# Sixteen pairs of heads in one line: making the next pair's keys and values beside the scores, and writing the maxima into the score banks with ScalarE

## The chip, the core and the metric

The kernel runs on one core of a Trainium2 chip. Its time is the device time of one execution in microseconds. The core has five engines that work side by side and meet only at semaphores: TensorE (PE in the profile) multiplies matrices, VectorE (DVE), ScalarE (ACT) and GpSimd (POOL) work on elements, and SyncE (SP) issues the transfers. TensorE writes to the eight banks of PSUM, each 512 float32 wide on 128 partitions; GpSimd cannot read them, DVE and ACT can.

## The reference, cut to what matters

The whole computation is a four-layer model with cross attention, self attention and a feed-forward part in each layer. The change touches only the cross attention of layer 1: 2 batches of 256 latent rows attend to 4096 context rows and to the latents themselves, with 16 heads of width 64.

```python
x = layer_norm(x, ln_m_g, ln_m_b)                # context: 2 x 4096 x 256
lat = layer_norm(latents, ln_l_g, ln_l_b)        # 2 x 256 x 256
q = lat @ Wq                                     # 256 -> 1024 = 16 heads of 64
kv = jnp.concatenate([x, lat], axis=1) @ Wkv     # 4352 keys and values
k, v = jnp.split(kv, 2, axis=-1)
q, k, v = (split_heads(q), split_heads(k), split_heads(v))
dots = jnp.einsum('bhid,bhjd->bhij', q, k) * scale
attn = jax.nn.softmax(dots, axis=-1)
out = jnp.einsum('bhij,bhjd->bhid', attn, v)
return out.transpose(0, 2, 1, 3).reshape(b, m, heads * dim_head) @ Wout
```

## The kernel before, in words

`latent_attention` (L1324) does the part between the queries and the normalized averages. It loops twice over the batch (`Fori`, L1363), each turn of the loop a stage of its own with a barrier at its end. In a turn there are four groups of four heads, that is, of two pairs of heads; a pair fills the 128 partitions with two heads of 64. A group has two phases.

In the **fill phase** TensorE makes 18 key tiles (`tile`, L1474: two pairs of heads, nine blocks of up to 512 keys) and 17 value tiles (L1479: 256 keys by four heads). ACT copies each out of PSUM (L1588, L1591). GpSimd casts the keys to bfloat16 (L1410). Between the tiles TensorE makes coarse scores from bfloat16 keys and queries (`peak_products`, L1453) into two sets of two banks, and DVE reduces each set to the maximum of every query (`read_peaks`, L1629). The maxima of a pair of heads are turned into a row by TensorE (`peak_rows`, L1492), and DVE copies the row to `mrow` (L1639).

In the **score phase** the group has 34 steps, 17 for each pair of heads, taken two at a time. A step has 256 keys: TensorE first writes the negative maxima into two score banks with two bfloat16 matmuls of a row of ones and `mrow` (L1509), adds the float32 scores on top (L1515), ACT takes the exponential over 1024 columns (L1605), and TensorE multiplies the result by the values (`average`, L1532). DVE (L1651) and GpSimd (L1421) each add one head's exponentials up, and at a pair's end TensorE sums them over partitions (`denominators`, L1545). `normalize` (L1658, L1659) divides. The averages of the preceding two steps come behind the scores of the present two.

The order is written out by hand, engine by engine. The score banks `pss` hold the tiles of the fill phase too, so the two phases of a group cannot overlap. In front of all this a small stage clears `mrow` (L1352), and each turn of the loop begins with 20 idle matmuls (`keep_busy`, L106). Afterwards `project_residual` (L309) multiplies by the output weights.

Of the kernel before, what the change touches and what calls it, by code (L numbers as in the profile page):

```python
# [14 lines left out]
ALU = mybir.AluOpType  # L15
# [1308 lines left out]
def latent_attention(nc, k, d, pre, OT):  # L1324
# [3 lines left out]
    hd, KEYS, GROUPS, RING = HD64, CTX + S, 4, 4  # L1328
    KT = KEYS // P
    SCALE = float(hd) ** -0.5  # L1330
    NQ = [(j * 512, min(512, KEYS - j * 512)) for j in range((KEYS + 511) // 512)]
    NB = len(NQ)
    NK, NV = KC * NB, KT // 2
    TILES = NK + NV
    STEPS = KT // 2
    ALL = KC * STEPS
    PEAKS = KC * NB
    QEV = 2 * KC

    names = ("c_load0 c_load1 c_load2 c_load3 latents nt_here wq_load wk_load wv_load q_mm q_ev tile_mm tile_ev k_cast peaks peak_read peak rows row_in "  # L1340
             "scored exps averaged sum_dve sum_pool den o_done chain").split()
    with Tensors(nc) as t:
        cT = t.sb(pre + "_cT", [P, KC, KEYS])
        V = t.sb(pre + "_V", [P, KT, 4, hd])
        K = t.sb(pre + "_K", [P, KC, KEYS])
        Kb = t.sb(pre + "_Kb", [P, KC, KEYS], BF16)
        Qb = t.sb(pre + "_Qb", [P, 2, KC, S], BF16)
        mrow = t.sb(pre + "_mrow", [P, KC, 2, S], BF16)
        with stage(nc, pre + "_fill", pre + "_fill1") as (block, _u, _v):
            @block.gpsimd  # L1350
            def _(pool):
                nc.gpsimd.memset(mrow[:, :, :, :], 0.0)  # L1352

        with nc.Fori(0, B) as b:
            with Tensors(nc) as u, stage(nc, *[pre + "_" + n for n in names], repeated=True) as (block, *sems):
                (c_load0, c_load1, c_load2, c_load3, latents, nt_here, wq_load, wk_load, wv_load, q_mm, q_ev, tile_mm, tile_ev, k_cast, peaks, peak_read, peak, rows, row_in,
                 scored, exps, averaged, sum_dve, sum_pool, den, o_done, chain) = sems
                c_loads = (c_load0, c_load1, c_load2, c_load3)
                CL = CTX // 4
                w = u.sb(pre + "_w", [P, 3, KC, D])  # L1360
                nt = u.sb(pre + "_nt", [P, KC, S])
                Q = u.sb(pre + "_Q", [P, 2, KC, S])
                pk = u.sb(pre + "_pk", [P, KC, QT, 2, NB])  # L1363
                mx = u.sb(pre + "_mx", [P, KC, 4])
                acc = u.sb(pre + "_acc", [P, 2, 2, 2, S])
                pr = u.sb(pre + "_pr", [P, RING, 2, 2, S])
                rec = u.sb(pre + "_rec", [P, S])
                pss = u.ps(pre + "_pss", [P, 4, 512])
                psm = u.ps(pre + "_psm", [P, 2, 512])
                pso = u.ps(pre + "_pso", [P, 512])  # L1370
                pst = u.ps(pre + "_pst", [P, 512])

                def averages_of(n):
                    return pso[:, 0:S] if n == 0 else psm[:, 1, 0:S]

                def peaks_by(t_):

                    if t_ < 2:
                        return 0
                    return min(PEAKS, -(-PEAKS * (t_ - 1) // (TILES - 2)))  # L1380

                def peak_banks(qt):
                    return psm[:, :, :] if qt == 0 else pss[:, 2:4, :]

                @block.sync
                def _(sp):
                    for g in range(GROUPS):
                        if g >= 1:
                            sp.wait_ge(q_mm, g)
                        sp.dma_start(w[:, 0, :, :], d[pre + "_w3"][g][:, 0]).then_inc(wq_load, 16)  # L1390
                        if g >= 1:
                            sp.wait_ge(tile_mm, TILES * (g - 1) + NK)
                        sp.dma_start(w[:, 1, :, :], d[pre + "_w3"][g][:, 1]).then_inc(wk_load, 16)
                        if g == 0:
                            for x in range(4):
                                sp.dma_start(cT[:, :, x * CL:(x + 1) * CL], k.normedT[b][:, :, x * CL:(x + 1) * CL]).then_inc(c_loads[x], 16)
                        if g >= 1:
                            sp.wait_ge(tile_mm, TILES * g)
                        sp.dma_start(w[:, 2, :, :], d[pre + "_w3"][g][:, 2]).then_inc(wv_load, 16)

                @block.gpsimd
                def _(pool):
                    nc.gpsimd.tensor_copy(nt[:, :, :], k.NT[:, :, bass.ds(b * S, S)]).then_inc(nt_here, 1)
                    nc.gpsimd.tensor_copy(cT[:, :, CTX:KEYS], k.NT[:, :, bass.ds(b * S, S)]).then_inc(latents, 1)
                    for g in range(GROUPS):
                        for n in range(NK):
                            m, j = divmod(n, NB)
                            o, w_ = NQ[j]
                            pool.wait_ge(tile_ev, TILES * g + n + 1)
                            nc.gpsimd.tensor_copy(Kb[:, m, o:o + w_], K[:, m, o:o + w_]).then_inc(k_cast, 1)  # L1410
                        for a in range(ALL):
                            n, s = divmod(a, STEPS)
                            A, U = ALL * g + a, KC * g + n
                            pool.wait_ge(exps, A + 1)
                            if s == 0:
                                if U >= 2:
                                    pool.wait_ge(den, U - 1)
                                i = nc.gpsimd.tensor_copy(acc[:, n, 1, :, :], pr[:, A % RING, :, 1, :])
                            else:
                                pool.wait_ge(sum_pool, A)  # L1420
                                i = nc.gpsimd.tensor_tensor(acc[:, n, 1, :, :], acc[:, n, 1, :, :], pr[:, A % RING, :, 1, :], ALU.add)  # L1421
                            i.then_inc(sum_pool, 1)

                @block.tensor
                def _(pe):
                    def queries(g):
                        pe.wait_ge(wq_load, 16 * (g + 1))
                        if g == 0:
                            pe.wait_ge(nt_here, 1)
                        else:  # L1430
                            pe.wait_ge(peak_read, QT * PEAKS * g)
                        for m in range(KC):
                            for c in range(KC):
                                i = nc.tensor.matmul(psm[:, 0, m * S:(m + 1) * S], w[:, 0, c, m * P:(m + 1) * P], nt[:, c, :],
                                                     start=(c == 0), stop=(c == KC - 1))
# [2647 lines left out]
```

## Time and profile before

| what | value |
|---|---|
| median of 3 runs | 3688.89 us (3686.14 to 3690.83) |
| span of the profiled execution | 3677.2 us |
| median less span | 11.7 us |
| the changed part: first queries to the last denominators' end | 599.12 to 1812.25 us |
| TensorE busy in the span | 92% |

The profiled execution's own time is given only as its span, from the first instruction to the last; the median of the timed runs lies 11.7 us above it. "Granted clock" is the share of TensorE's full clock that the chip let it have in a stretch. Busy time of TensorE is modelled: a matmul's duration covers its way through the array, so the distance between the starts of two groups of matmuls says what one costs, and the duration printed does not. A float32 matmul shows as two records.

### The profile page before, as it was taken

To read this page: it belongs to the slowest core of one execution; us is meant where nothing else is said; L and a number is where in the kernel's file an instruction comes from. 1 tells how busy PE (TensorE), PEld (TensorE's weight loads), DVE (VectorE), ACT (ScalarE), POOL (GpSimd) and SP (SyncE) were. 2 spreads that over 40 slices of the span, in tenths; PEclk is the share of its full clock that TensorE was granted. 3 is DMA by queue.
4 is the path that set the end of the run, shared out by engine and by line. 5 is a ranking of instruction groups with operands and counts; after the bars stand their busy time and mean duration, and the time that the engine had idled before them with its cause. 6 is when DMAs were issued, how large, how long until landed. Compare 5 with 4: busy or idle time off the path is not lost. (4 is left out here: it accounts for less than half of the span.)

```text
span 3677.2 us, 56678 instructions
## 1 busy us (share of the span) xinstructions
PE 3396.7 (92%) x22589; PEld 2130.7 (58%) x22608; DVE 2126.4 (58%) x3378; ACT 1525.3 (41%) x2294; POOL 904.2 (25%) x665
## 2 busy tenths in 40 slices
PE   8989898999999999999967888999988889999899
PEld 5855695655656556565634576444455644445575
DVE  4335313555555555555468621999855279995654
ACT  2335211424334243343355522466745137665621
POOL 1032001426345163452517512000011120000430
PEclk9999999999999999999988999999999989999999
DMA  5358562000000100000097533756500386550010
GB/s 190 105 188 273 186 249 84 7 6 5 7 1 1 61 7 9 4 4 1 12 241 281 206 143 120 190 117 121 101 26 24 124 226 125 117 106 22 1 48 36
DMA packets 228860, 346.91 MB, mean 94 GB/s; under 512 B 104176, under 2 KB 177584, under 8 KB 223984
## 3 DMA queue, kind: packets, MB, share of 16 engines
q1 hardware_dynamic: 228208, 342.16, 32.1%
q8 instruction: 184, 3.01, 0.3%
q0 software_dynamic: 384, 1.05, 0.1%
q14 instruction: 84, 0.69, 0.1%
HBM read 257.15 MB, written 86.02 MB: 93 GB/s over the span
## 5 line engine op out<-in xcount | busy, mean ns | idle before, releaser
L1421 POOL TENSOR_TENSOR L1x_acc<-L1x_acc,L1x_pr 128x512 f32<-128x512 f32 x256 | 418.0, 1633 | 135.7 <-ACT L1x_pr L1605 117.4
L1605 ACT ACTIVATE L1x_pr<-L1x_pss 128x1024 f32<-128x1024 f32 x272 | 278.4, 1024 | 288.2 <-PE L1x_pss L1515 280.5
L1651 DVE TENSOR_TENSOR L1x_acc<-L1x_acc,L1x_pr 128x512 f32<-128x512 f32 x256 | 255.4, 997 | 213.2 <-ACT L1x_pr L1605 209.4
L1234 DVE TENSOR_REDUCE L3x_pk<-L3x_psm 128x1 f32<-128x512 f32 x512 | 328.8, 685 | 25.9 <-PE L3x_psm L1063 19.4
L1234 DVE TENSOR_REDUCE L2x_pk<-L2x_psm 128x1 f32<-128x512 f32 x512 | 328.8, 685 | 20.7 <-PE L2x_psm L1063 14.1
L1211 ACT ACTIVATE L3x_pr<-L3x_pss 128x1024 f32<-128x1024 f32 x256 | 248.1, 1021 | 106.3 <-PE L3x_pss L1106 106.0
L1211 ACT ACTIVATE L2x_pr<-L2x_pss 128x1024 f32<-128x1024 f32 x256 | 248.1, 1021 | 102.0 <-PE L2x_pss L1106 101.8
L1629 DVE TENSOR_REDUCE L1x_pk<-L1x_psm 128x2 f32<-128x1024 f32 x144 | 168.0, 1167 | 211.1 <-PE L1x_psm L1453 211.1
L1515 PE MATMUL L1x_pss<-L1x_Q,L1x_K 64*128 64x256 f32 x2176 | 279.3, 376 | 0.0
L1479 PE MATMUL L1x_pss<-L1x_w,L1x_cT 128*128 128x256 f32 x1088 | 257.5, 387 | 0.0
L1474 PE MATMUL L1x_pss<-L1x_cT,L1x_w 128*128 128x512 f32 (+1 forms) x576 | 256.4, 584 | 0.5 <-DMA L1x_cT<-normed_context 0.5
L1479 PEld LDWEIGHTS L1x_pss<-L1x_w,L1x_cT 128*128 128x128 f32 x1088 | 200.1, 190 | 54.6 <-issue 27.2
L1515 PEld LDWEIGHTS L1x_pss<-L1x_Q,L1x_K 64*128 64x128 f32 x2176 | 208.4, 188 | 36.0
L2894 POOL TENSOR_SCALAR s_qz<-s_qT,s_mask 128x256 f32<-128x256 f32 x64 | 58.3, 918 | 652.1 <-SPq L58 433.8
L3876 POOL TENSOR_TENSOR o_pr<-o_h,m_cr 128x1024 f32<-128x1024 f32 x31 | 72.8, 2355 | 504.1 <-DVE o_h L3955 504.1
L1588 ACT COPY L1x_K<-L1x_pss 128x512 f32<-128x512 f32 x144 | 80.8, 561 | 257.5 <-PE L1x_pss L1474 257.5
L1474 PEld LDWEIGHTS L1x_pss<-L1x_cT,L1x_w 128*128 128x128 f32 x576 | 102.4, 189 | 120.8 <-issue 110.2
L1591 ACT COPY L1x_V<-L1x_pss 128x512 f32<-128x512 f32 x136 | 79.6, 585 | 217.9 <-PE L1x_pss L1479 217.9
L1629 DVE TENSOR_REDUCE L1x_pk<-L1x_pss 128x2 f32<-128x1024 f32 x144 | 166.5, 1156 | 0.0
L841 PE MATMUL n_psk<-n_cT,n_w 128*128 128x512 f32 x256 | 125.7, 616 | 37.0 <-DMA n_cT<-in_ctxT 36.9
L879 ACT ACTIVATE n_kst<-n_psk,n_b 128x512 bf16<-128x512 f32 x192 | 121.6, 688 | 57.3 <-PE n_psk L841 47.7
L1410 POOL CAST L1x_Kb<-L1x_K 128x512 bf16<-128x512 f32 x144 | 84.9, 590 | 242.8 <-ACT L1x_K L1588 242.8
(742 smaller groups left out, 6126.7 us busy)
## 6 DMA issues: line engine op xcount, KB each, us to landing
f0e_wt<-in_f_pieces SPq DMA_DIRECT2D x10, 3072.0 KB, 11.5
offset_rows<-s_rows SPq DMA_DIRECT2D x32, 768.0 KB, 5.8
L2x_KS<-L2x_key_parts SPq DMA_DIRECT2D x24, 1024.0 KB, 12.8
L3x_KS<-L3x_key_parts SPq DMA_DIRECT2D x24, 1024.0 KB, 12.8
s_add<-offset_rows SPq DMA_DIRECT2D x32, 512.0 KB, 7.5
n_cT<-in_ctxT SPq DMA_DIRECT2D x32, 512.0 KB, 4.6
f1e_wt<-in_f_pieces SPq DMA_DIRECT2D x8, 2048.0 KB, 12.7
L2x_key_parts<-n_kst SPq DMA_DIRECT2D x32, 384.0 KB, 2.8
```

The costliest lines, as they stand in the source:

```text
L841: i = nc.tensor.matmul(cx.psk[:, n % 4, :], cx.w[:, l, 0, c, m * P:(m + 1) * P], cx.cT[:, q % CRING, c, :], start=(c == 0), stop=(c == KC ...
L879: nc.scalar.activation(cx.kst[:, q % SRING, m, part, :], cx.psk[:, n % 4, :], ACT.Identity, bias=cx.bias[:, mine[q][1], m:m + 1]).then_inc ...
L1211: nc.scalar.activation(pr[:, a % RING, :, :].rearrange("p h q -> p (h q)"), pss[:, 2 * (a % 2):2 * (a % 2) + 2, :].rearrange("p x q -> p ( ...
L1234: nc.vector.reduce_max(pk[:, n % 2, h * QT + qt, j:j + 1], psm[:, x % 3, :], AX).then_inc(turn_read, 1)
L1410: nc.gpsimd.tensor_copy(Kb[:, m, o:o + w_], K[:, m, o:o + w_]).then_inc(k_cast, 1)
L1421: i = nc.gpsimd.tensor_tensor(acc[:, n, 1, :, :], acc[:, n, 1, :, :], pr[:, A % RING, :, 1, :], ALU.add)
L1474: i = nc.tensor.matmul(pss[:, x, 0:w_], w[:, 1, c, m * P:(m + 1) * P], cT[:, c, o:o + w_], start=(c == 0), stop=(c == KC - 1))
L1479: i = nc.tensor.matmul(pss[:, x, c * D:(c + 1) * D], cT[:, e, kt * P:(kt + 1) * P], w[:, 2, e, :], start=(e == 0), stop=(e == KC - 1))
L1515: i = nc.tensor.matmul(pss[:, x + h, e * S:(e + 1) * S], K[half, n, kt * P:(kt + 1) * P], Q[half, g % 2, n, :], start=False, stop=True, sk ...
L1605: nc.scalar.activation(pr[:, A % RING, :, :, :].rearrange("p h e q -> p (h e q)"), pss[:, x:x + 2, :].rearrange("p h n -> p (h n)"), ACT.E ...
L1629: nc.vector.reduce_max(pk[:, m, qt, :, j], peak_banks(qt)[:, :, 0:NQ[j][1]], AX).then_inc(peak_read, 1)
L1651: i = nc.vector.tensor_tensor(acc[:, n, 0, :, :], acc[:, n, 0, :, :], pr[:, A % RING, :, 0, :], ALU.add)
```

## The change

`latent_attention` is written anew as one stage without the loop. The eight groups of both batches form one line of 136 pairs of steps. Beside each pair of steps TensorE now makes one key tile (11 tiles ahead of use, `KLEAD`), one value tile (9 ahead, `VLEAD`) and the coarse scores of one key tile. The last key blocks of two pairs of heads share one tile (`KL`), so a group has 17 key tiles. The two bfloat16 matmuls that wrote the maxima are gone: TensorE spreads the negative maxima over all partitions once for each pair of heads (`spread_rows`, a matmul of ones with diagonal matrices that DVE makes), ACT copies them to `neg`, and `seed` has ACT write `neg` into the two score banks before each step. The key tile has PSUM bank 0 of `psm`, the value tile bank 2; the coarse scores of the first 128 queries use banks 0 and 1, those of the other 128 banks 1 and 2. The small clearing stage is gone.

```diff
-    hd, KEYS, GROUPS, RING = HD64, CTX + S, 4, 4
-        with nc.Fori(0, B) as b:
-                def averages_of(n):
-                    return pso[:, 0:S] if n == 0 else psm[:, 1, 0:S]
+    hd, RING, GROUPS = HD64, 4, B * 4
+    KLEAD, VLEAD, VRING, BRING = 11, 9, SLOTS + 2, 3
+        def read_in(p):
+            z = p + KLEAD - 1
+            return z if z < TILES else None
+        def peak_banks(z, qt):
+            return psm[:, qt:qt + 2, :] if z >= KLEAD - 1 else pss[:, 2 * qt:2 * qt + 2, :]
...
# TensorE
-                        for h in range(2):
-                            half = slice(64 * h, 64 * h + 64)
-                            nc.tensor.matmul(pss[:, x + h, :], k.onesb[half, :], mrow[half, n, :, :].rearrange("p e q -> p (e q)"),
-                                             start=True, stop=False, skip_group_check=True)
+            def spread_rows(u, bank):
+                pe.wait_ge(diag, u + 1)
+                nc.tensor.matmul(psm[:, bank, :], k.onesb[:, :], dm[:, :, :, :].rearrange("p h t q -> p (h t q)"), start=True, stop=True).then_inc(rows, 1)
+            def scores(a):
+                u, s = unit_of(a)
+                g, m = divmod(u, KC)
+                pe.wait_ge(seeded, a + 1)
...
+            for z in range(KLEAD):
+                key_tile(z)
+                if z >= KLEAD - VLEAD:
+                    value_tile(z - KLEAD + VLEAD)
+                if z >= 1:
+                    pe.wait_ge(k_cast, z)
...
+                    for qt in range(QT):
+                        peak_products(z - 1, qt)
+            pe.wait_ge(k_ev, KLEAD - 1)
+            spread_rows(0, 1)
+            for p in range(PAIRS):
+                z = read_in(p)
+                def first_peaks():
+                    if z is not None:
+                        pe.wait_ge(k_cast, z + 1)
+                        pe.wait_ge(peak_read, QT * z)
...
+                        peak_products(z, 0)
+                def second_peaks():
+                    if z is not None:
+                        pe.wait_ge(peak_read, QT * z + 1)
+                        pe.wait_ge(v_ev, VLEAD + 1 if p == 0 else min(TILES, p + VLEAD))
...
+                        peak_products(z, 1)
+                def tiles():
+                    if keys_in(p) is not None:
+                        key_tile(keys_in(p))
+                    if values_in(p) is not None:
+                        if p >= 1:
+                            pe.wait_ge(peak_read, QT * min(TILES, p + KLEAD))
+                        value_tile(values_in(p))
...
+                first_peaks()
+                scores(2 * p)
+                scores(2 * p + 1)
+                second_peaks()
+                if p > 0:
+                    tiles()
...
+                for a in averages_in(p):
+                    average(a)
# ScalarE
+            def seed(a):
...
+                nc.scalar.copy(pss[:, x:x + 2, :].rearrange("p h (e q) -> p h e q", e=2),
+                               neg[:, u % 2, :, :].unsqueeze(2).broadcast_to([P, 2, 2, S])).then_inc(seeded, 1)
...
+                exponentials(2 * p)
+                exponentials(2 * p + 1)
+                if p + 1 < PAIRS:
+                    act.wait_ge(exps, 2 * p + 1)
+                    seed(2 * p + 2)
+                if p > 0 and keys_in(p) is not None:
+                    evict_keys(keys_in(p))
+                if p + 1 < PAIRS:
+                    act.wait_ge(exps, 2 * p + 2)
+                    seed(2 * p + 3)
+                if p > 0 and values_in(p) is not None:
+                    evict_values(values_in(p))
# GpSimd
+            for p in range(PAIRS):
+                sum_step(2 * p)
+                sum_step(2 * p + 1)
+                if keys_in(p) is not None:
+                    cast(keys_in(p))
# VectorE
+            for p in range(PAIRS):
+                z = read_in(p)
+                if z is not None:
+                    read_peaks(z, 0)
...
+                if z is not None:
+                    read_peaks(z, 1)
+                    diagonals(z)
+                sum_step(2 * p)
+                sum_step(2 * p + 1)
```

This is TensorE's line before, in the score phase of a group. `L1x_pss` are the score banks, `mrow` the maxima, `pr` the exponentials.

```order
L1509 MATMUL L1x_pss<-L1x_mrow,ones_bf 128x512 x2
L1515 MATMUL L1x_pss<-L1x_Q,L1x_K 128x256 x4
L1509 MATMUL L1x_pss<-L1x_mrow,ones_bf 128x512 x2
L1515 MATMUL L1x_pss<-L1x_Q,L1x_K 128x256 x4
L1532 MATMUL L1x_pso<-L1x_pr,L1x_V 64x256 x8
```

These five rows are one pair of steps; the tiles stand in another stretch of the same line. This is TensorE's line after, one pair of steps in the middle of the line and the first two rows of the next. `L1x_psm` holds tiles and coarse scores.

```order
L1525 MATMUL L1x_psm<-L1x_Kb,L1x_Qb 128x512 x2
L1542 MATMUL L1x_pss<-L1x_Q,L1x_K 128x256 x8
L1525 MATMUL L1x_psm<-L1x_Kb,L1x_Qb 128x512 x2
L1501 MATMUL L1x_psm<-L1x_cT,L1x_w 128x512 x2
L1516 MATMUL L1x_psm<-L1x_w,L1x_cT 128x256 x4
L1555 MATMUL L1x_pso<-L1x_pr,L1x_V 64x256 x8
L1525 MATMUL L1x_psm<-L1x_Kb,L1x_Qb 128x512 x2
L1542 MATMUL L1x_pss<-L1x_Q,L1x_K 128x256 x8
```

The writing of the maxima is gone from TensorE, and coarse scores (L1525), a key tile (L1501) and a value tile (L1516) stand inside every pair of steps. On ScalarE a group was this before, 18 key copies, 17 value copies and then 34 exponentials without anything between them:

```order
L1588 COPY L1x_K<-L1x_pss 128x512 x8
L1588 COPY L1x_K<-L1x_pss 128x256
L1588 COPY L1x_K<-L1x_pss 128x512 x8
L1588 COPY L1x_K<-L1x_pss 128x256
L1591 COPY L1x_V<-L1x_pss 128x512 x17
L1605 ACTIVATE L1x_pr<-L1x_pss 128x1024 x34
```

One pair of steps on ScalarE now, with the exponentials of the next pair behind it:

```order
L1671 ACTIVATE L1x_pr<-L1x_pss 128x1024 x2
L1661 COPY L1x_pss<-L1x_neg 128x1024
L1646 COPY L1x_K<-L1x_psm 128x512
L1661 COPY L1x_pss<-L1x_neg 128x1024
L1650 COPY L1x_V<-L1x_psm 128x512
L1671 ACTIVATE L1x_pr<-L1x_pss 128x1024 x2
```

Two copies over 1024 columns into PSUM (L1661) are new in each pair of steps, and the two tile copies stand between and behind them.

## Rows read from the trace of the kernel before

**Rows 1.** The page: busy time and share of the span of each engine.

```profile
PE 3396.7 (92%) x22589; PEld 2130.7 (58%) x22608; DVE 2126.4 (58%) x3378; ACT 1525.3 (41%) x2294; POOL 904.2 (25%) x665
```

**Rows 2.** Windows: stretch, length, busy of PE, PEld, DVE, ACT, POOL, granted clock.

```profile
600.00:676.00 76.00, 73.56 (x295) 40.87 (x294) 43.80 (x46) 20.05 (x35) 10.62 (x18) 1.00 0.13 50
676.00:753.00 77.00, 76.95 (x642) 49.37 (x644) 39.14 (x42) 35.98 (x36) 54.70 (x36) 1.00 0.03 8
```

**Rows 3.** Timeline (start, duration, engine) of TensorE: one pair of steps.

```profile
689.46 1.95 PE L1532 MATMUL L1x_pso<-L1x_pr,L1x_V 128*64 128x256 f32 x16
691.34 0.39 PE L1509 MATMUL L1x_pss<-L1x_mrow,ones_bf 64*128 64x512 bf16 x2
691.57 1.03 PE L1515 MATMUL L1x_pss<-L1x_Q,L1x_K 64*128 64x256 f32 x8
...
693.61 1.95 PE L1532 MATMUL L1x_pso<-L1x_pr,L1x_V 128*64 128x256 f32 x16
```

**Rows 4.** Timeline of TensorE: fill phase, value tiles and coarse scores.

```profile
656.78 3.72 PE L1479 MATMUL L1x_pss<-L1x_w,L1x_cT 128*128 128x256 f32 x16
660.43 0.39 PE L1453 MATMUL L1x_psm<-L1x_Kb,L1x_Qb 64*128 64x512 bf16 x2
...
660.97 3.72 PE L1479 MATMUL L1x_pss<-L1x_w,L1x_cT 128*128 128x256 f32 x16
```

**Rows 5.** Timeline of TensorE: from the first turn of the loop to the second.

```profile
1199.00 2.27 PE L106 MATMUL L1x_pss<-ident 128*128 128x128 f32 x18
...
1213.12 1.89 PE L1434 MATMUL L1x_psm<-L1x_nt,L1x_w 128*128 128x256 f32 x8
1214.85 5.31 PE L1474 MATMUL L1x_pss<-L1x_cT,L1x_w 128*128 128x512 f32 x12
1220.10 0.39 PE L1453 MATMUL L1x_psm<-L1x_Kb,L1x_Qb 64*128 64x512 bf16 x2
```

**Rows 6.** Timeline of all engines: a wait of TensorE for DVE's reads.

```profile
606.86 0.39 PE L1453 MATMUL L1x_psm<-L1x_Kb,L1x_Qb 64*128 64x512 bf16 x2
607.29 1.23 DVE L1629 TENSOR_REDUCE L1x_pk<-L1x_psm 128x2 f32<-128x1024 f32 x1 [4.82 <-PE L1x_psm L1453]
608.43 1.22 DVE L1629 TENSOR_REDUCE L1x_pk<-L1x_pss 128x2 f32<-128x1024 f32 x1
609.79 0.39 PE L1453 MATMUL L1x_psm<-L1x_Kb,L1x_Qb 64*128 64x512 bf16 x2 [0.42 <-DVE L1x_pk L1629]
```

**Rows 7.** Timeline of all engines: exponentials and sums of two steps.

```profile
885.82 1.03 PE L1515 MATMUL L1x_pss<-L1x_Q,L1x_K 64*128 64x256 f32 x8
886.89 2.10 ACT L1605 ACTIVATE L1x_pr<-L1x_pss 128x1024 f32<-128x1024 f32 x2 [2.04 <-PE L1x_pss L1515]
887.95 0.69 DVE L1651 TENSOR_TENSOR L1x_acc<-L1x_acc,L1x_pr 128x512 f32<-128x512 f32 x1 [1.77 <-ACT L1x_pr L1605]
888.00 3.45 POOL L1421 TENSOR_TENSOR L1x_acc<-L1x_acc,L1x_pr 128x512 f32<-128x512 f32 x2 [0.69 <-ACT L1x_pr L1605]
```

**Rows 8.** Tile `L1x_acc`: durations in ns, least, median, greatest.

```profile
L1651 DVE TENSOR_TENSOR L1x_acc<-L1x_acc,L1x_pr x256: 691/693/1579, 679.4 to 1808.7; 128x512 f32<-128x512 f32 x128
L1421 POOL TENSOR_TENSOR L1x_acc<-L1x_acc,L1x_pr x256: 1263/1536/1786, 679.5 to 1809.6; 128x512 f32<-128x512 f32 x128
```

**Rows 9.** Groups by line: tile copies, casts.

```profile
L1410 POOL CAST L1x_Kb<-L1x_K 128x512 bf16<-128x512 f32 x144 | 84.9, 590 | 242.8 <-ACT L1x_K L1588 242.8
L1588 ACT COPY L1x_K<-L1x_pss 128x512 f32<-128x512 f32 x144 | 80.8, 561 | 257.5 <-PE L1x_pss L1474 257.5
```

**Rows 10.** Timeline: the small stage, the start and the end of the changed part.

```profile
591.54 0.95 POOL L1352 MEMSET L1x_mrow<- 128x1024 bf16 x1 [15.10 <-POOLq L58]
...
599.12 1.89 PE L1434 MATMUL L1x_psm<-L1x_nt,L1x_w 128*128 128x256 f32 x8
...
601.53 5.39 PE L1474 MATMUL L1x_pss<-L1x_cT,L1x_w 128*128 128x512 f32 x12 [0.52 <-DMA L1x_cT<-normed_context]
...
1812.25 2.27 PE L106 MATMUL L1x_pss<-ident 128*128 128x128 f32 x18
```

More of the change, by code:

```diff
@@ L1324, in latent_attention @@
 def latent_attention(nc, k, d, pre, OT):
-    hd, KEYS, GROUPS, RING = HD64, CTX + S, 4, 4
-    KT = KEYS // P
-    SCALE = float(hd) ** -0.5
[L1331 to L1341, printed above, removed]
@@ new lines, in latent_attention @@
+    hd, RING, GROUPS = HD64, 4, B * 4
+    UNITS = KC * GROUPS
+    KT = (CTX + S) // P
+    STEPS = KT // 2
+    NBLK = CTX // 512
+    SLOTS = STEPS
+    ALL = STEPS * UNITS
+    PAIRS, TILES = ALL // 2, SLOTS * GROUPS
+    KLEAD, VLEAD, VRING, BRING = 11, 9, SLOTS + 2, 3
+    SCALE = float(hd) ** -0.5
+    OF_W = 16 * 3
+    names = ("c_here0 c_here1 c_here2 c_here3 c_here4 c_here5 c_here6 c_here7 w_here q_mm q_ev k_mm k_ev v_mm v_ev k_cast peaks peak_read diag rows row_in "
+             "seeded scored exps averaged o_copied sum_dve sum_pool den den_read o_done chain").split()
```

621 lines of the change are left out of this document (319 added, 302 removed).

## The prediction

> **What bounds the kernel now.** I read the page first: TensorE is busy 92% of the span, no other engine above 58% [rows 1]. The windows of the changed part say the same of each phase: in a fill phase TensorE is busy 73.6 of 76 us at granted clock 1.00 (the upper level, 2.4 GHz), in a score phase 76.95 of 77 us; ACT has 20 and 36 us, DVE 44 and 39, GpSimd 11 and 55 [rows 2]. So TensorE bounds both phases, and the change is worth what it takes from TensorE's line, provided that no other engine becomes late in the new, denser order. The rows are then read by the distance between starts, because that is what a piece costs on TensorE.
>
> **What the pieces cost.** A pair of steps takes 693.61 - 689.46 = 4.15 us: averages A 1.88, and 2.27 for two times maxima and scores. One writing of maxima is 691.57 - 691.34 = 0.23, so the scores S of two steps take 2.27 - 0.46 = 1.81, with a change of array mode behind them [rows 3]. The coarse scores P of one block take 660.97 - 660.43 = 0.54, which is two pieces of 0.23 and 0.08 for the change from 64-row mode to whole-array mode [rows 4]. Eight whole-array records followed by others of that mode take 1214.85 - 1213.12 = 1.73 (a key tile has the same number of columns; three of them with the change behind take 5.25, or 1.75 each) [rows 5]. Two value tiles take 660.43 - 656.78 = 3.65 with the change behind, so a last value tile V takes 1.92 [rows 4].
>
> **A pair of steps after the change.** P in two parts 0.54, S 1.73 (1.81 less the 0.08 for a change of mode that no longer follows, since P's second part has the scores' mode), key tile K 1.73, V 1.92, A 1.88: 7.80 us. By the old phases, without looking at joints, it would be 4.15 - 0.46 + 0.54 + 3.65 = 7.88. The cheapest reading drops the change between V and A, 1.73 in place of 1.92: 7.61. I take 7.80.
>
> The trace prices a change of array mode at 0.08 us behind coarse scores and 0.19 behind value tiles [rows 4, 5]. The Trainium skill, TensorEngine Tiling (Array Packing), Key Properties, says that changing the mode drains TensorE. It speaks against a line that changes mode inside every pair. By it one counts: before, two changes in a score pair and two around a coarse block, four; after, A to P, P to K and V to A, three. The Trainium skill has no price for it; without the rule the sum would go by 7.88 and end 10 us higher, at 3589.
>
> **Does anything else get late inside 7.80 us?** Let a pair start at 0 with P's first part. S runs 0.23 to 1.96, P's second part to 2.27, K to 4.00, V to 5.92, A to 7.80.
> - *DVE.* The second part of P shares a bank with the first and waits for its read. A read starts 0.43 after the matmuls, takes 1.23, and TensorE goes on 0.14 after its end (607.29 - 606.86; 609.79 less 608.43 + 1.22) [rows 6]: 1.80, against 1.96, a slack of 0.16. V waits likewise: 1.96 + 1.80 = 3.76 against 4.00. Then come two sums of 0.69 to 1.58 [rows 8], done by 3.62 + 3.16 = 6.8 at the latest. It is the tightest place.
> - *ACT.* An exponential starts 1.07 after its scores' first matmul and takes 1.05 (886.89 - 885.82, two in 2.10) [rows 7]: 1.30 to 3.40, in time for A at 5.92. The two seeds have no row: ACT writes nothing into PSUM before. Below, the half-width copy out of PSUM, 0.56 [rows 9]; above, the dearest element work of that kind at full width, twice an exponential, 2.1; I take 1.05, since the exponential has the same 128x1024 [rows 7]. Then seed to 4.45, key copy to 5.0, seed to 6.1, value copy to 6.7. The second scores of the next pair want the second seed at 7.80 + 1.10 = 8.9: seeds up to 2.4 us cost nothing, so neither end of that bound is on the path.
> - *GpSimd.* Two sums take 3.45 [rows 7] from 2.37 on, to 5.8, the cast 0.59 [rows 9], to 6.4. The next pair's P waits for that cast at 7.80. Slack 1.4.
> - *SP* brings the second batch's context in eight parts, each seven or more pairs (55 us) before its key tile, so the wait at the loop's second turn goes. No DMA is queued behind another that is due sooner.
> - Diagonals of DVE (16 times), the queries' copies and the copy of the denominators have a pair's slack each; I cost them at nothing, and at most 0.5 us x 32 = 16 us if they meet P's read.
>
> **The sum, from first queries to last denominators.** Queries and the wait for the context 2.4 (601.53 - 599.12) [rows 10]. Ahead of the first scores 11 K, 9 V, 10 P: 1.73, 2.46 and 9 x 4.19, 41.9. Hand-over: one matmul that spreads the row, K, V, and a wait for ACT, which makes two seeds only after the last coarse read: reads end 2.8 after P's start, seeds 2.1, key copy 0.6, against 0.54 + 0.3 + 3.65 of TensorE: 1.2; together 5.2. The rest of pair 0: 4.2. Pairs 1 to 124: 124 x 7.80 = 967.2. Pair 125 has no K, 6.1, pair 126 no K and P, 5.5. The last nine have scores and averages only, 3.6 of TensorE, but ACT has two exponentials and two seeds, 4 x 1.05 + 0.1: 9 x 4.3 = 38.7; 2.0 for the last averages. Seven more queries of 1.73, 12.1; 16 denominators at half of A, 15.0; 15 spread rows of 0.25, 3.8. Total 1104.1 us. Before it is 1812.25 - 599.12 = 1213.1 [rows 10]. Difference -109.0. The clearing stage (a memset of 0.95) goes, -1.0; its bounds are 0 and -2. At the end the denominators are copied by ACT before the reciprocal, +0.5. In all -109.5.
>
> Where it comes from: 272 writings of maxima of 0.23 (62), the loop's seam of 1213.12 - 1199.00 = 14.1 [rows 5], the coarse blocks reduced by eight and the rows made by eight small matmuls (about 10), the fill phases' own waits (the 76 - 73.6 of a fill, eight times, 19), a change of mode per pair (10), less what ACT holds up at the end (6) and the hand-over.
>
> The span would be 3677.2 - 109.5 = 3567.7. The profiled execution's own time is not given beside its span; the median is 11.7 above the span, so the forecast is **3579 us**.
>
> **Rivals.**
> - *The reads of the maxima wait in view.* The slack of 0.16 is a difference of modelled ends. If a read starts late or takes longer beside ACT's writes, P's second part and V wait. At +0.35 per pair: 125 x 0.35 = 44, 3623. For it: DVE already made TensorE wait 0.42 there, though in another order [rows 6]. Against it: in a pair DVE has 5.6 us at the most for 7.8.
> - *The joints are cheap.* A pair of 7.61: 125 x 0.19 = 24 less, 3555. For it: whole-array and column-split mode may follow each other without a loss, which no row shows by itself; against it: A itself shows 1.88 where its columns match 1.73.
> - *GpSimd slowed by DVE: slower.* GpSimd's sums grow, since DVE is now busy most of the time, and the cast, queued behind both sums on GpSimd, comes late for P, on whose heels everything hangs. It decides from 7.80 - 2.37 - 0.59 - 0.1 = 4.7 us for two sums on; the kernel is slower than before from a pair of 7.80 + 109.5 / 124 = 8.68 on, that is, sums of 2.8 each. At 3.3 each the pair is 9.66: 125 x 1.86 = 232 more, less 109.5, 3811. For it: GpSimd's sums range from 1.26 to 1.79 and DVE's from 0.69 to 1.58 beside each other [rows 8]. Against it: 1.79 is the most in 256, with both at work. The Trainium skill, SBUF — State Buffer, Who interferes with whom, says that a DVE instruction with at most one SBUF input outside its two-port modes does not contend with GpSimd, while one with two does. The added DVE work beside the sums is reads of PSUM, so by the Trainium skill this rival is nearly out; the trace has no reads beside GpSimd's sums to show it.
> - *It is not what it says:* ACT's own waits between exponential and seed (it waits for its own exponential's end) could cost some tenths each, but ACT has 2.4 us free per pair; that leaves 3579 as it is, but for the last nine pairs, +3.
>
> **Chances.** Forecast 0.74 (own range 3565 to 3597, pairs of 7.70 to 7.93), reads in view 0.13, joints cheap 0.08, GpSimd 0.03, something not seen 0.02. The range 3558 to 3622 leaves out GpSimd's case and the far half of the first rival. A measurement of this kernel can tell 0.2%, 7.4 us, from no change. Faster: 0.95; same 0.01; slower 0.04.
>
> **What would show it.** In the timeline of the new kernel pairs start 7.7 to 7.9 apart, TensorE is busy over 97% from the first key tile to pair 126, at clock 1.00, ACT copies of 128x1024 into the score banks take 1.0 to 1.1, nobody waits for them before the last nine pairs, and those are 4.3 apart. Waits of TensorE put down to DVE's reduction of more than 0.1 each would show the first rival; waits put down to GpSimd's cast, the third. The forecast is wrong if pairs are over 8.0 apart or the last nine far over 4.3.

## The result, and the profile after

The changed kernel takes 3577.78 us (median of 4; 3571.99 to 3585.08) against 3687.51 us (4 runs) before: a ratio of 0.971, 95% interval 0.9695 to 0.9724, 110 us less. Forecast were 3579 us. Timed again beside the experiments it was 3580.21, ratio 0.970 (0.9685 to 0.9716).

The windows of the profile after: ahead of the changed part, the part from its first queries to its last denominators, and behind it (columns as in [rows 2], then DMA share and GB/s).

```profile
0.00:602.59 602.59, 533.72 (x3131) 407.46 (x3131) 222.85 (x619) 173.27 (x381) 83.49 (x92) 0.97 0.54 187
602.59:1709.68 1107.09, 1095.87 (x6800) 693.54 (x6800) 698.07 (x718) 688.57 (x848) 492.36 (x408) 1.00 0.04 13
1709.68:3583.30 1873.62, 1689.28 (x11966) 1008.78 (x11964) 1243.69 (x2073) 910.87 (x1360) 301.52 (x152) 0.95 0.44 117
```

The part takes 1107.1 us, 106.0 less than the 1213.1 between the rows of before [rows 10]; 1104.1 were forecast. TensorE is busy for 99% of it at clock 1.00, ACT for 62% (688.6). A pair of steps in the middle of the line, in the timeline of all engines but TensorE's weight loads:

```profile
1011.86 0.39 PE L1525 MATMUL L1x_psm<-L1x_Kb,L1x_Qb 64*128 64x512 bf16 x2
1012.09 1.89 PE L1542 MATMUL L1x_pss<-L1x_Q,L1x_K 64*128 64x256 f32 x16
1012.30 1.23 DVE L1730 TENSOR_REDUCE L1x_pk<-L1x_psm 128x2 f32<-128x1024 f32 x1 [0.18 <-PE L1x_psm L1525]
1013.17 1.94 ACT L1671 ACTIVATE L1x_pr<-L1x_pss 128x1024 f32<-128x1024 f32 x2 [2.49 <-PE L1x_pss L1542]
1013.82 0.38 PE L1525 MATMUL L1x_psm<-L1x_Kb,L1x_Qb 64*128 64x512 bf16 x2
1014.13 1.98 PE L1501 MATMUL L1x_psm<-L1x_cT,L1x_w 128*128 128x512 f32 x4
1014.27 2.94 POOL L1464 TENSOR_TENSOR L1x_acc<-L1x_acc,L1x_pr 128x512 f32<-128x512 f32 x2 [3.81 <-ACT L1x_pr L1671]
1014.99 1.03 ACT L1661 COPY L1x_pss<-L1x_neg 128x1024 f32<-128x1024 f32 x1
1015.38 2.38 DVE L1760 TENSOR_TENSOR L1x_acc<-L1x_acc,L1x_pr 128x512 f32<-128x512 f32 x2
1015.95 1.89 PE L1516 MATMUL L1x_psm<-L1x_w,L1x_cT 128*128 128x256 f32 x8
1016.15 0.58 ACT L1646 COPY L1x_K<-L1x_psm 128x512 f32<-128x512 f32 x1
1016.63 1.02 ACT L1661 COPY L1x_pss<-L1x_neg 128x1024 f32<-128x1024 f32 x1
1017.16 1.07 POOL L1450 CAST L1x_Kb<-L1x_K 128x512 bf16<-128x512 f32 x1
1017.77 1.95 PE L1555 MATMUL L1x_pso<-L1x_pr,L1x_V 128*64 128x256 f32 x16
1019.65 0.39 PE L1525 MATMUL L1x_psm<-L1x_Kb,L1x_Qb 64*128 64x512 bf16 x2
```

Read the starts of TensorE's rows: 0.23 for P's first part, 1.73 for the scores, 0.31, key tile 1.82, value tile 1.82, averages 1.88, in all 7.79. No row of TensorE carries a wait in brackets. ACT's two seeds (L1661) stand ahead of the key copy and behind it, 1.03 and 1.02, and its next exponential comes 2.5 us after its last work. Where [rows 3] had 0.23 twice per pair for the maxima, there is nothing on TensorE.

The hand-over from the lead to the first pairs, and the last pairs, in TensorE's timeline:

```profile
646.11 0.39 PE L1531 MATMUL L1x_psm<-L1x_dm,ones_bf 128*128 128x512 bf16 x1
...
650.92 0.39 PE L1525 MATMUL L1x_psm<-L1x_Kb,L1x_Qb 64*128 64x512 bf16 x2 [0.98 <-ACT L1x_K L1646]
...
653.74 2.00 PE L1555 MATMUL L1x_pso<-L1x_pr,L1x_V 128*64 128x256 f32 x16 [0.49 <-ACT L1x_pr L1671]
...
657.06 0.39 PE L1525 MATMUL L1x_psm<-L1x_Kb,L1x_Qb 64*128 64x512 bf16 x2 [1.32 <-POOL L1x_Kb L1450]
...
1657.99 1.99 PE L1516 MATMUL L1x_psm<-L1x_w,L1x_cT 128*128 128x256 f32 x8 [1.32 <-DVE L1x_pk L1730]
...
1681.89 2.00 PE L1542 MATMUL L1x_pss<-L1x_Q,L1x_K 64*128 64x256 f32 x16
1684.15 2.00 PE L1555 MATMUL L1x_pso<-L1x_pr,L1x_V 128*64 128x256 f32 x16 [0.26 <-ACT L1x_pr L1671]
1686.08 2.00 PE L1542 MATMUL L1x_pss<-L1x_Q,L1x_K 64*128 64x256 f32 x16
```

Pair 0 waits three times, 2.8 us in all. Pair 125 has no key tile between P's second part and its value tile, and there the wait for DVE's read comes into view, 1.32. The last pairs are 1686.08 - 1681.89 = 4.19 apart.

### The profile page after: what moved, and what is told of

It reads as the page before. It is cut to its first block and busy times, and to the rows that moved or that the text cites. A ratio compares the mean times of both kernels' runs of the same rounds, so it can differ in the third digit from the quotient of the medians.

```text
span 3583.3 us, 56143 instructions
## 1 busy us (share of the span) xinstructions
PE 3318.9 (93%) x21894; PEld 2109.8 (59%) x21894; DVE 2164.6 (60%) x3410; ACT 1772.7 (49%) x2589; POOL 877.4 (24%) x652
## 3 DMA queue, kind: packets, MB, share of 16 engines
q0 software_dynamic: 384, 1.05, 0.1%
## 5 line engine op out<-in xcount | busy, mean ns | idle before, releaser
L1464 POOL TENSOR_TENSOR L1x_acc<-L1x_acc,L1x_pr 128x512 f32<-128x512 f32 x256 | 357.6, 1397 | 538.6 <-ACT L1x_pr L1671 521.4
L1730 DVE TENSOR_REDUCE L1x_pk<-L1x_psm 128x2 f32<-128x1024 f32 x238 | 291.7, 1226 | 318.9 <-PE L1x_psm L1525 318.9
L1661 ACT COPY L1x_pss<-L1x_neg 128x1024 f32<-128x1024 f32 x272 | 278.5, 1028 | 1.3 <-DVE L1x_pk L1730 1.3
L1555 PE MATMUL L1x_pso<-L1x_pr,L1x_V 128*64 128x256 f32 x2176 | 265.3, 386 | 2.6 <-ACT L1x_pr L1671 2.6
L1501 PE MATMUL L1x_psm<-L1x_cT,L1x_w 128*128 128x512 f32 x512 | 253.4, 618 | 0.0
L1516 PE MATMUL L1x_psm<-L1x_w,L1x_cT 128*128 128x256 f32 x1024 | 242.0, 379 | 1.3 <-DVE L1x_pk L1730 1.3
L1516 PEld LDWEIGHTS L1x_psm<-L1x_w,L1x_cT 128*128 128x128 f32 x1024 | 194.5, 190 | 79.0 <-issue 30.2
L1555 PEld LDWEIGHTS L1x_pso<-L1x_pr,L1x_V 128*64 128x64 f32 x2176 | 143.4, 136 | 107.1 <-issue 40.7
L1501 PEld LDWEIGHTS L1x_psm<-L1x_cT,L1x_w 128*128 128x128 f32 x512 | 87.0, 189 | 113.1 <-issue 112.8
L1106 PE MATMUL L2x_pss<-L2x_QS,L2x_KS 97*128 97x256 bf16 x1024 | 138.1, 277 | 0.6
```

Of the source, the lines that this page charges most:

```text
L1106: i = nc.tensor.matmul(pss[:, 2 * (a % 2) + h // 2, h % 2 * S:(h % 2 + 1) * S], KS[0:ONE + 1, n % 2, h, s * P:(s + 1) * P], QS[0:ONE + 1, ...
L1501: i = nc.tensor.matmul(psm[:, x, :], w[:, g % 2, 1, c, m * P:(m + 1) * P], cT[:, c, j * 512:(j + 1) * 512], start=(c == 0), stop=(c == KC ...
L1516: i = nc.tensor.matmul(psm[:, 2, h * D:(h + 1) * D], keys, w[:, g % 2, 2, c, :], start=(c == 0), stop=(c == KC - 1))
L1555: i = nc.tensor.matmul(pso[64 * h:64 * h + 64, 0:S], V[:, (SLOTS * g + s) % VRING, e, 2 * n + h, :], pr[:, a % RING, h, e, :], start=(s == ...
L1661: nc.scalar.copy(pss[:, x:x + 2, :].rearrange("p h (e q) -> p h e q", e=2), neg[:, u % 2, :, :].unsqueeze(2).broadcast_to([P, 2, 2, S])).t ...
L1730: nc.vector.reduce_max(pk[:, m, qt, :, j], peak_banks(z, qt), AX).then_inc(peak_read, 1)
```

## The experiments

The theory: TensorE bounds every full pair; the seeds gain because they leave TensorE where ACT has room; the seam and the fill phases' waits make up the rest. Lengths of the part are read from each run's trace as above (first queries to last denominators' end); they repeat closely (1107.1 in both profiles of the changed kernel), while the rest of the program varies by 20 us from one profiled execution to another (2458.8 to 2479.1). Each ratio is taken to the kernel before as timed beside that run (3684.05 to 3687.77 us). Edits are shown in part; `...` in them marks lines left out.

| run | us | ratio to before (95%) | length of the part |
|---|---|---|---|
| before | 3687.51 | | 1213.1 |
| changed | 3577.78 | 0.971 (0.9695 to 0.9724) | 1107.1 |
| e0 changed, again | 3580.21 | 0.97 (0.9685 to 0.9716) | 1107.1 |
| e1 line, maxima by TensorE | 3631.75 | 0.9852 (0.9835 to 0.987) | 1158.4 |
| e2 two phases, seeds, half the maxima of a group's first steps lost | 3699.54 | 1.0032 (1.0021 to 1.0044) | 1231.3 |
| e2b the same, all maxima kept | 3707.4 | 1.0054 (1.0033 to 1.0074) | 1230.9 |
| e3 DVE's read late | 3587.87 | 0.9731 (0.971 to 0.9752) | 1119.4 |
| e4 seeds twice | 3608.23 | 0.9783 (0.9754 to 0.9811) | 1140.2 |
| e5 a line per batch | 3599.38 | 0.9765 (0.9742 to 0.9788) | 1128.1 |
| e6 both ends changed | 3581.22 | 0.9712 (0.9694 to 0.9729) | 1108.8 |
| e7 GpSimd late | 3724.68 | 1.011 (1.0085 to 1.0135) | 1255.1 |
| e8 tail: averages late, DVE seed | 3579.05 | 0.9697 (0.9679 to 0.9716) | 1107.9 |
| e9 tail: averages late | 3580.43 | 0.971 (0.969 to 0.973) | 1106.9 |

**The changed kernel again.** 

> The changed kernel once more, beside the others on the same chip. Expected 3573 to 3585 us, as in its four runs; the distance between its time and its span 1.8 us as in them, which would put the 11.7 us of the prediction down to the spread between executions.

It came as expected; its profiled execution took 3581.13 us with a span of 3579.4, so 1.7 us lie around the span.

**e1: half of the change, the line without the seeds.**

```diff
-                pe.wait_ge(seeded, a + 1)
...
+                if a >= 2:
+                    pe.wait_ge(exps, a - 1)
+                for h in range(2):
+                    half = slice(64 * h, 64 * h + 64)
+                    nc.tensor.matmul(pss[:, 2 * (a % 2) + h, :], k.onesb[half, :], mrow[half, u % 2, :, :].rearrange("p e q -> p (e q)"),
+                                     start=True, stop=False, skip_group_check=True)
...
```

> The changed line, but the maxima are written into the score banks by two bfloat16 matmuls per step again, and ACT makes no seeds (half of the change). Theory: TensorE bounds every pair, so 272 x 0.23 = 62 us come back, less about 1 at the hand-over; pairs 8.24 apart in place of 7.78; 3638 us. Rival: overlap is what gained and the seeds on ACT only kept even; then 3578 to 3590.

Two pairs' first rows in TensorE's timeline:

```profile
1036.35 0.39 PE L1526 MATMUL L1x_psm<-L1x_Kb,L1x_Qb 64*128 64x512 bf16 x2
1036.57 0.38 PE L1543 MATMUL L1x_pss<-L1x_mrow,ones_bf 64*128 64x512 bf16 x2
...
1044.56 0.39 PE L1526 MATMUL L1x_psm<-L1x_Kb,L1x_Qb 64*128 64x512 bf16 x2
```

8.21 apart, 0.43 more than 7.78: 125 such pairs are 54 us, and the part is 51.3 longer; 3638 us was expected and 3631.75 measured. The 14 pairs with a row of maxima grow only from 8.35 to 8.53. The theory's mechanism holds, at 0.22 a step in place of 0.23; the rival, that the seeds only kept even, falls.

**e2 and e2b: the other half alone, seeds in the two-phase kernel.**

```diff
# TensorE's scores
...
-                            nc.tensor.matmul(pss[:, x + h, :], k.onesb[half, :], mrow[half, n, :, :].rearrange("p e q -> p (e q)"),
-                                             start=True, stop=False, skip_group_check=True)
+                        pe.wait_ge(seeded, ALL * g + a + 1)
# ScalarE, behind each second exponential
+                            if a % 2 == 1 and a + 1 < ALL:
+                                act.wait_ge(exps, A)
+                                seed(g, a + 1)
+                                act.wait_ge(exps, A + 1)
+                                seed(g, a + 2)
# e2b only: the value tile's second half starts without the flag
-                                                         start=(e == 0), stop=(e == KC - 1))
+                                                         start=(e == 0 and c == 0), stop=(e == KC - 1), skip_group_check=True)
...
```

> The kernel before with its loop and its two phases, but ACT writes the maxima into the score banks (the other half of the change). Theory: a pair of steps of the score phase has 3.7 us of TensorE, but two exponentials and two seeds on ACT, 4.19, which is what a pair takes before (4.15); the seeds gain nothing there, and each group adds a seed of 1.03 between the last tile and the first scores: 3690 us, from 3685 to 3700. Rival: what leaves TensorE is gained wherever it leaves: 62 us less, 3626.

> The kernel of e2 with one flag changed so that the first steps of a group keep their maxima (in e2 half the columns of each group's first steps lost them); the work and its order are the same. Theory: the same time as e2, 3697 to 3707, slower than the kernel before by 10 to 20 us, with pairs 4.12 apart; what TensorE no longer does there is not gained. Rival: the lost maxima had changed the time; then another number than e2's.

The timeline of all engines in e2b, first scores of a group and, further down, a pair in the middle:

```profile
678.54 1.96 ACT L1569 COPY L1x_pss<-L1x_neg 128x1024 f32<-128x1024 f32 x2
679.61 2.08 PE L1496 MATMUL L1x_pss<-L1x_Q,L1x_K 64*128 64x256 f32 x16 [1.72 <-ACT L1x_pss L1569]
...
683.73 3.68 PE L1496 MATMUL L1x_pss<-L1x_Q,L1x_K 64*128 64x256 f32 x16 [2.04 <-ACT L1x_pss L1569]
...
707.66 2.00 PE L1496 MATMUL L1x_pss<-L1x_Q,L1x_K 64*128 64x256 f32 x16
708.84 1.94 ACT L1598 ACTIVATE L1x_pr<-L1x_pss 128x1024 f32<-128x1024 f32 x2 [1.99 <-PE L1x_pss L1496]
710.66 1.97 ACT L1569 COPY L1x_pss<-L1x_neg 128x1024 f32<-128x1024 f32 x2
711.75 2.07 PE L1496 MATMUL L1x_pss<-L1x_Q,L1x_K 64*128 64x256 f32 x16 [0.21 <-ACT L1x_pss L1569]
```

Pairs of plain score steps are 4.11 to 4.12 apart, as good as the 4.15 of before [rows 3]: 0.45 us less of TensorE's work is given back as waits for ACT: 0.2 ahead of the scores of each pair, and 0.2 again for the weight loads of the second step. At a group's start TensorE waits 1.72 and 2.04 in the group shown. From the last value tile's start to the first averages' start a group takes 9.84 to 11.45 us, against 7.32 in all eight before: about 24 us more in sum, where one seed of 1.03 for each group, 8 us, was expected. That is most of why 3707.4 us came out and not 3690. The lost maxima of e2 changed nothing in the time of the part (1231.3 and 1230.9).

The edit has one more piece: the last coarse block of a pair of heads is 512 keys wide in place of 256, which by the distance from the block to the next value tile (0.53 in place of 0.32) makes an estimated 3 us (16 x 0.21) of the 18 by which the part is longer. So the seeds are worth +14 to +18 us in the two phases and -51 us in the line (1107.1 against 1158.4).

**e3: a later read by DVE.**

```diff
+                if z >= KLEAD and qt == 0:
+                    nc.vector.tensor_copy(spare[:, :], psm[:, 0, 0:S])
                 if j < NBLK:
```

> The changed kernel with one more DVE copy of 128x256 out of PSUM (0.34 us from start to next start) ahead of the read that the second part of the coarse scores waits for, in each of the 125 pairs. If the slack of that read is the 0.15 us that the trace shows, each pair grows by 0.19: 24 us, 3602, and the second part of P waits for DVE in every pair. Rival: the slack is larger than its modelled ends say: 3578. Or there is none, and all 0.34 show: 3621.

TensorE and DVE in one pair:

```profile
1009.47 0.39 PE L1526 MATMUL L1x_psm<-L1x_Kb,L1x_Qb 64*128 64x512 bf16 x2
...
1010.24 1.22 DVE L1733 TENSOR_REDUCE L1x_pk<-L1x_psm 128x2 f32<-128x1024 f32 x1
...
1011.52 0.39 PE L1526 MATMUL L1x_psm<-L1x_Kb,L1x_Qb 64*128 64x512 bf16 x2
```

P's second part starts 2.05 after the first, in place of 1.96, and 0.06 after the read's end. The pair is 7.88 to 7.89, 0.10 longer, and the part 12.3. Of the 0.34 added 0.24 were slack: the slack was real, small, and larger than the 0.15 expected, so that 3587.87 us came out in place of 3602. The changed kernel's own rows agree: the read ends at 1013.53 and P's second part starts at 1013.82; less the 0.06 that is 0.23.

**e4: seeds twice.**

```diff
+                nc.scalar.copy(pss[:, x:x + 2, :].rearrange("p h (e q) -> p h e q", e=2),
+                               neg[:, u % 2, :, :].unsqueeze(2).broadcast_to([P, 2, 2, S])).then_inc(once, 1)
+                act.wait_ge(once, a + 1)
                 nc.scalar.copy(...).then_inc(seeded, 1)
```

> The changed kernel with each seed written twice by ACT, one after the other. Theory: up to 2.4 us a seed costs nothing beside a full pair, so pairs stay 7.78 apart; only the last nine pairs grow, by 2.1 to 2.3 each, and the hand-over by 2 to 3: 3600 us. Rival: ACT is near the path already and the pairs grow by 1 us or more: 3700 and up.

```profile
1014.22 0.39 PE L1525 MATMUL L1x_psm<-L1x_Kb,L1x_Qb 64*128 64x512 bf16 x2
...
1017.34 1.03 ACT L1661 COPY L1x_pss<-L1x_neg 128x1024 f32<-128x1024 f32 x1
...
1018.41 1.02 ACT L1664 COPY L1x_pss<-L1x_neg 128x1024 f32<-128x1024 f32 x1
...
1022.00 0.39 PE L1525 MATMUL L1x_psm<-L1x_Kb,L1x_Qb 64*128 64x512 bf16 x2
```

The plain pairs stay at 7.78 to 7.80: two more microseconds of ACT beside them are free. The part is 33.1 longer, not 22: pairs with one more duty on the row of maxima come to 8.84 in place of 8.35 (14 of them, 7 us), seven with denominators to 9.36 in place of 8.65 (5 us). From pair 125 on it takes 72.1 in place of 55.4, 16.7 more, with plain tail pairs at 6.2; the other 4 or so are at the start, from the first queries to pair 2.

**e5: a line per batch.**

```diff
+    for b in range(B):
+        one_line(nc, k, d, pre, OT, b)
...
-    hd, RING, GROUPS = HD64, 4, B * 4
+    hd, RING, GROUPS = HD64, 4, 4
```

> The changed kernel, but the line is cut into two of 8 head pairs, one for each batch, each a stage with its own lead and its own end. Theory: the seam costs about what it cost before, 14 us, and a second hand-over (2.8), a second set of nine pairs bound by ACT (5) come with it: 22 us, 3600. Rival: the single line is the larger part of the gain: 3630 and up.

```profile
1156.46 2.27 PE L106 MATMUL L1x_pss<-ident 128*128 128x128 f32 x18
1159.57 4.70 PE L106 MATMUL L1x_pss<-ident 128*128 128x128 f32 x40 [0.83 <-PEq L58]
1164.11 1.89 PE L1481 MATMUL L1x_psm<-NT,L1x_w 128*128 128x256 f32 x8
1167.18 3.67 PE L1500 MATMUL L1x_psm<-L1x_cT,L1x_w 128*128 128x512 f32 x8 [1.18 <-DMA L1x_cT<-normed_context]
```

The part is 21.0 longer, where 22 were expected. The seam itself is 7.7 us (1164.11 - 1156.46), about half of what the loop's took [rows 5]; a wait for the context (1.18), a second hand-over and a second tail make up the rest, more than was expected for them, so the total came right with its parts off. In the one line the seam costs nothing: with what comes along it is 21 of the 106 us.

**e7: GpSimd late.**

```diff
+                    for e in range(2):
+                        nc.gpsimd.tensor_tensor(spare[:, e, :, :], k.NT[:, 0, :].rearrange("p (e q) -> p e q", e=2), k.NT[:, 1, :].rearrange("p (e q) -> p e q", e=2), ALU.add)
                     cast(keys_in(p))
```

> The changed kernel with two more additions of 128x512 on GpSimd (1.0 to 1.5 us each) between its sums and the cast in each of the 125 pairs. By the trace the cast has 1.3 us to spare; so each pair grows by 0.7 to 1.7, 90 to 210 us: 3670 to 3790 us, and the coarse scores wait for the cast. Rival: the cast is not waited for so closely and nothing changes, 3578.

GpSimd and TensorE at the end of a pair:

```profile
1062.56 2.95 POOL L1475 TENSOR_TENSOR L1x_spare<-NT 128x512 f32<-128x512 f32 x2
1065.46 0.61 POOL L1451 CAST L1x_Kb<-L1x_K 128x512 bf16<-128x512 f32 x1
...
1066.12 0.39 PE L1528 MATMUL L1x_psm<-L1x_Kb,L1x_Qb 64*128 64x512 bf16 x2 [1.03 <-POOL L1x_Kb L1451]
```

Plain pairs are mostly 8.88 apart, 1.10 longer (some others reach 10.5 to 12.1, so that the part is 148 longer), and the kernel is slower than before. That is the forecast's slower rival made by hand: past the cast's slack everything added on GpSimd is added to the time. The 2.9 us added, less 1.4 of slack (the cast ends at 1018.23, P starts at 1019.65) and the 0.46 by which the cast became shorter, are 1.1.

**e6, e8, e9: the ends.**

```diff
# e6: GpSimd casts the next key tile ahead of the first sums; ACT copies it out between the first two seeds;
# in the last nine pairs:
+                if TAIL <= 2 * p + 3 < ALL:
+                    seed_by_dve(2 * p + 3)
...
# e9: averages a pair late in the last pairs; e8: that, and seed_by_dve in the last six
+            if p >= PAIRS - 7:
+                return [2 * p - 2, 2 * p - 1] if p > PAIRS - 7 else []
```

> The changed kernel with its two ends mended: at the hand-over GpSimd casts the next key tile before the first sums and ACT copies it out between the two seeds, and in the last nine pairs DVE makes the second seed. Theory: pair 0 loses about 1 us in place of 2.8, the last nine pairs come down from 4.19 to about 3.8: 5 us less than the changed kernel, 3573, too little to be told from it in the times but visible in the trace. Rival: DVE's seed takes longer than ACT's and the last nine stay at 4.2 or rise.

> The changed kernel with two edits in its last pairs: the averages stand behind the next pair's scores (as in the kernel before), and DVE makes the second seed. After e6, where the last pairs kept 4.19 us though ACT had 1.33 free, the theory is that they are bound by a chain: scores, first exponential, averages, next scores, on TensorE in that order. With the averages a pair late the chain is broken, and with a seed taken from ACT TensorE's own 3.7 us are left: about 0.45 us less in each of the last six pairs, 3 us, 3577. Rival: something else holds these pairs and they stay at 4.19.

> The same with the averages late alone; ACT makes both seeds. Theory: the chain is broken, but ACT's own four instructions take 1.94 + 1.97 and two joints, so the last pairs come to 4.0 to 4.1 in place of 4.19, under 1 us in all; ACT no longer sits idle in them. Rival: 3.7, which would say that ACT's load was never a bound there.

In e6, two tail pairs of ACT, TensorE and DVE:

```profile
1692.70 1.94 ACT L1677 ACTIVATE L1x_pr<-L1x_pss 128x1024 f32<-128x1024 f32 x2 [1.33 <-PE L1x_pss L1548]
1693.78 2.00 PE L1561 MATMUL L1x_pso<-L1x_pr,L1x_V 128*64 128x256 f32 x16 [0.26 <-ACT L1x_pr L1677]
...
1694.68 1.23 DVE L1774 COPY L1x_pss<-L1x_neg 128x1024 f32<-128x1024 f32 x1 [0.23 <-ACT L1x_pr L1677]
1695.71 2.00 PE L1548 MATMUL L1x_pss<-L1x_Q,L1x_K 64*128 64x256 f32 x16
...
1696.89 1.94 ACT L1677 ACTIVATE L1x_pr<-L1x_pss 128x1024 f32<-128x1024 f32 x2 [1.33 <-PE L1x_pss L1548]
```

ACT now idles 1.33 us per pair and the pair is still 4.19, where 3.8 was expected. (One pair takes 5.90: TensorE waits 1.50 there for DVE's seed. That is the 1.7 by which this part is longer than the changed kernel's.) It is a ring: scores to exponential 1.18, first exponential and its signal 1.08, averages 1.93, scores again, 4.19. In e8 the averages are out of that ring, and the timeline shows the next one:

```profile
1694.41 1.94 ACT L1681 ACTIVATE L1x_pr<-L1x_pss 128x1024 f32<-128x1024 f32 x2 [1.23 <-PE L1x_pss L1550]
...
1696.23 1.03 ACT L1671 COPY L1x_pss<-L1x_neg 128x1024 f32<-128x1024 f32 x1
...
1697.32 2.00 PE L1550 MATMUL L1x_pss<-L1x_Q,L1x_K 64*128 64x256 f32 x16 [0.21 <-ACT L1x_pss L1671]
...
1698.50 1.94 ACT L1681 ACTIVATE L1x_pr<-L1x_pss 128x1024 f32<-128x1024 f32 x2 [1.23 <-PE L1x_pss L1550]
```

Both exponentials and the seed 2.85, to the scores 0.06, scores to exponential 1.18: 4.09. I expected 3.7, and that fails. e9 gave 4.11, against 4.0 to 4.1 expected, with ACT's idle time down to 0.29, though not gone. None of the three is measurably faster than the changed kernel (1106.9 to 1108.8 against 1107.1), and at the hand-over e6 only moved the wait: its first averages wait 1.43 for the exponential. A seed ahead of the second exponential might shorten the ring of e8; it wasn't tried and isn't shown. By an estimate from 4.19 and the 3.7 of TensorE's work the whole tail is worth about 3 us.

## Why the prediction was right, and where it was not

**The pair.** Forecast 7.80, measured 7.78 or 7.79 in 82 of the first 125 pairs, the others having an extra duty or one average less. Its pieces are off against each other: the key tile takes 1.82, not 1.73 (behind P it pays for the change of mode as well), the value tile 1.82, not 1.92. The sum was robust because it came from measured blocks with their joints in them. The rule that a change of mode drains TensorE, from the Trainium skill, TensorEngine Tiling (Array Packing), Key Properties, agrees with the trace: behind each of the three changes left in a pair the next group starts 0.31 after the start of the last matmuls, against 0.21 to 0.22 where the mode stays, and the first matmul of the key tile takes 0.53 from start to start in place of 0.43. The step by the old phases, 7.88, was 0.10 too high. The rival with cheap joints, 7.61, falls.

**What hides the seeds.** They took 1.03 where 1.05 was taken, and e4 doubles them without moving a plain pair. e2b shows the condition: where ACT has only the 4.15 us of the old score pair, the seeds gain nothing. The change is one only as a whole: in the length of the part the halves alone give +18 (e2b) and -55 us (e1), both together -106.

**DVE's read.** The slack of 0.16 was priced right in kind; e3 measures 0.24. The step's error is the 0.14 between a read's end and TensorE's start, which is 0.06 in e3's row. The first rival came true only in pair 125 (1.32).

**GpSimd.** The cast was taken at 0.59; beside DVE's sums it takes 1.07 (0.935 in the mean, against 0.590 [rows 9]), while GpSimd's own sums came down to a mean of 1.40 from 1.63. Slack 1.4, as forecast. e7 shows that the rival's price was of the right kind. The pairs of 7.78 show that its condition did not hold here.

**The other terms,** measured against forecast: start 1.8 (2.4), lead 41.7 (41.9), hand-over 4.8 (5.2), pair 0 6.1 (4.2), pairs 1 to 124 with their extras 997.3 (996.0), from pair 125 on 55.4 (54.5). Pair 0 was missed because I let it pass at 7.80 less its tiles: the averages wait for the exponential, and the cast stands behind both sums. The spread rows take 0.57 in place of 0.25 (8.35 less 7.78), partly a wait of 0.2 for DVE's diagonals. The four of them take 2.1 us beside GpSimd's sums and cast, against 0.74 in e2b, where GpSimd stands idle: the first takes 1.2 to 1.3 and ends 0.05 behind the end of GpSimd's sum. The prediction had costed them at nothing. The denominators take 0.87 in place of 0.94. The sum of all is 3.0 us.

Just outside the part the forecast had -1.0 for the clearing stage and +0.5 for the copy of the denominators. Measured in the two profiles are -1.7 (from the last idle matmuls of the stage ahead to the first queries 9.54 us before, 7.84 after) and -0.6 (from the start of the idle matmuls behind the denominators to the output projection 3.75 before, 3.11 after). So 1.8 of the 3.0 us are given back. The first of the two varies: in the other kernels with a line it is up to 1.4 shorter still.

**Where the gain comes from.** Of the 106 us 51 belong to the seeds (e1) and 21 to the one line in place of two (e5). The other 34, which the forecast gave to the coarse blocks, the fill phases' own waits and the changes of mode, no run takes apart.

**The tail** is right in number (4.19 for 4.3) by luck, and wrong in cause: the step said that ACT's four instructions bind it. They take 3.79 us of a pair, not 4.3, and ACT is nearly full there, but e6 takes a quarter of its load away and the pair does not move; a ring through TensorE's order of scores and averages has the same length. The changed kernel's own timeline shows that ACT was not the bound, since it still waits in each plain tail pair:

```profile
1687.26 1.94 ACT L1671 ACTIVATE L1x_pr<-L1x_pss 128x1024 f32<-128x1024 f32 x2 [0.40 <-PE L1x_pss L1542]
```

**From span to time** the step fails: 11.7 us do not lie around the span. In each profiled run of the changed kernel the time is 1.7 or 1.8 us above its span (3585.08 and 3583.3, 3581.13 and 3579.4). The profiled execution of before is not out of line with that: outside the part it took 2464.1 us, within the 2459 to 2479 of all the profiles here. With the median run's rest and the measured part it comes out alike, since a difference was added to a median; but about 10 of the 11.7 were spread between executions, not a cost. That forecast and median lie 1.2 us apart (3579 and 3577.78) is therefore luck: single executions of the changed kernel lie 13 us apart, and its second median is 3580.21. What the runs bear out is the length of the part, 1104.1 against 1107.1.

## What to carry to other kernels

An edit that moves work from a full engine to a free one is worth its time only if the free engine is free in that very stretch: the same seeds lengthened the part by 14 to 18 us in a phase where ACT stood at the pace of TensorE, and shortened it by 51 once the phases were interleaved and the pair twice as long. Sum a pipelined pair from blocks read start to start with their joints, then write beside it the time at which each other engine would be late; the smallest slack (here 0.24 us of DVE's read) is the next bound. Where two explanations give nearly the same length, as ACT's load (4.3 by the forecast) and the ring in the tail (4.19), only an edit that removes one of them tells which holds.

## What the hardware showed beside it

A copy of 128x1024 by ACT from SBUF into PSUM took 1.028 us in the mean of 272, an exponential of that size out of PSUM 1.021. The Trainium skill, ScalarE: Activation LUTs, Step-by-step: what each stage is for, says that writing to PSUM is the faster way for this engine; at this size no row here shows a difference, though the two also read from different memories.

GpSimd's cast grew from 0.61 to 1.07 when it ran beside DVE's sums, and was 0.61 again in e7, where it came behind them. This agrees with the rule of the Trainium skill, SBUF — State Buffer, Who interferes with whom, that a DVE instruction with two SBUF inputs contends with GpSimd; the reductions out of PSUM did not slow the sums of GpSimd: the 29 sums of the changed kernel that ran beside a reduction alone took 1.26 to 1.28, as did the eight beside neither, and the 116 beside DVE's sums alone had a median of 1.54. Two sums of a pair take 2.94 in place of 3.45 [rows 7].
